# One attention and int8 feed-forward layer on 8 cores: normalising block kg+1 ahead of the key/value work of block kg, or right before its own

## The reference, cut to what matters

```python
x = L0_attn_x                                  # (4, 4096, 2048) f32
x = x + layernorm(attn(layernorm(x)))
x = x + layernorm(ffn(layernorm(x)))

def attn(x, Wq, bq, Wdown, Wk_up, Wv_up, Wo, bo):   # 16 heads of 128
    q = x @ Wq + bq
    kv_latent = x @ Wdown                      # 2048 -> 512
    k = kv_latent @ Wk_up                      # 512 -> 2048
    v = kv_latent @ Wv_up
    ...                                        # rotary embedding on q and k
    scores = q k^T / sqrt(128), causal mask, softmax, times v
    return ctx @ Wo + bo

def ffn(x):                                    # int8 weights, 2048 -> 8192 -> 2048
    return qmatmul(silu(qmatmul(x, w_gate, s_gate)) * qmatmul(x, w_up, s_up),
                   w_down, s_down)
```

## Time and profile before

| what | us |
|---|---|
| runs shown: lowest, median, highest of 3 | 6573.32, 7085.65, 7111.39 |
| profiled execution, its time | 6567.78 |
| its span on the slowest core (core 3) | 6566.2 |
| its spans on all cores | 6519.4 to 6566.2 |

### The profile page before, as it was taken

One profiled execution on the slowest core, in us unless ns is written; L12 is line 12 of the kernel. 1 busy time (PEld: TensorE's weight loads), 2 busy tenths in 40 slices (PEclk: granted clock), 3 DMA queues, 4 the chain that ended last, 5 costly groups with the idle time before them and its releaser, 6 DMA issues.

```text
span 6566.2 us, 67793 instructions; the slowest of 8 cores (6519.4 to 6566.2 us)
## 1 busy us (share of the span) xinstructions
PE 4422.5 (67%) x21376; PEld 2017.3 (31%) x21376; DVE 1584.4 (24%) x2965; ACT 1349.6 (21%) x3067; POOL 818.8 (12%) x924
## 2 busy tenths in 40 slices
PE   0144334486666666663334999789986999879986
PEld 0011111132333334331111443334432444334432
DVE  0142334244333333323332110121102111021101
ACT  0212221111666666521111110010000110011100
POOL 0021112243000000000000111111111111111111
PEclk9867667798767776676666999989998999989998
DMA  9423333532777777764437996499946997489944
GB/s 180 114 77 109 90 95 90 126 79 78 153 147 150 147 148 147 149 151 128 140 119 144 154 154 136 120 177 151 154 129 153 151 151 137 128 161 151 160 119 131
DMA packets 1566328, 883.21 MB, mean 135 GB/s; under 512 B 777122, under 2 KB 1541026, under 8 KB 1550242
## 3 DMA queue, kind: packets, MB, share of 16 engines
q0 software_dynamic: 679296, 434.14, 39.1%
q1 hardware_dynamic: 839842, 327.28, 22.6%
q10 hardware_dynamic: 46848, 117.45, 5.3%
HBM read 398.53 MB, written 109.05 MB: 77 GB/s over the span
## 4 chain that ended last, share of the span: by engine, by line
PE 45%; DMA 19%; DVE 11%; ACT 10%; issue 8%; POOL 3%; SPq 2%; another core or an unknown queue 1%; ACTq 1%; DVEq 0%; POOLq 0%
PE ps L1031 14%; PE ps L1045 13%; PE ps L1098 7%; DMA arena<-wd 7%; ACT arena L766 7%; DMA ctxr<-xin 4%; PE ps L864 3%; PE ps L442 2%; PE ps L738 2%; DMA arena<-arena 2%; DVE smalls L760 2%; POOL arena L621 2%; PE ps L699 2%; DMA arena<-wo 1%; DVE arena L477 1%
## 5 line engine op out<-in xcount | busy, mean ns | idle before, releaser
L1031 PE MATMUL ps<-arena 128*128 128x512 bf16 x4096 | 936.2, 382 | 259.9 <-DMA arena<-wg 137.9
L1098 PE MATMUL ps<-arena 128*128 128x512 bf16 x4096 | 920.3, 380 | 140.1 <-DMA arena<-wd 138.7
L1045 PE MATMUL ps<-arena 128*128 128x512 bf16 x4096 | 925.8, 379 | 0.0
L766 ACT ACTIVATE arena<-ps,smalls 128x512 bf16<-128x512 f32 (+1 forms) x1152 | 748.9, 669 | 469.7 <-DVE smalls L760 322.8
L738 PE MATMUL ps<-arena 128*128 128x512 bf16 (+1 forms) x1152 | 488.3, 486 | 415.1 <-ACT arena L766 336.9
L1031 PEld LDWEIGHTS ps<-arena 128*128 128x128 bf16 x4096 | 403.0, 98 | 752.0 <-issue 275.6
L411 PE MATMUL ps<-arena 128*128 128x512 bf16 x512 | 130.4, 420 | 693.6 <-ACT arena L420 452.6
L1098 PEld LDWEIGHTS ps<-arena 128*128 128x128 bf16 x4096 | 385.7, 98 | 674.0 <-issue 246.5
L1061 DVE TENSOR_SCALAR ctxr<-ps,smalls 128x512 bf16<-128x512 f32 x256 | 192.1, 751 | 1498.7 <-PE ps L1045 1498.7
L1045 PEld LDWEIGHTS ps<-arena 128*128 128x128 bf16 x4096 | 400.8, 98 | 483.3
L1056 ACT ACTIVATE ctxr<-ps,smalls 128x512 bf16<-128x512 f32 x256 | 176.1, 688 | 1562.4 <-PE ps L1031 1562.3
(11 more groups left out here) (74 smaller groups left out, 2785.6 us busy)
## 6 DMA issues: line engine op xcount, KB each, us to landing
arena<-wg POOLq DMA_DIRECT2D x128, 1024.0 KB, 7.3
arena<-wu POOLq DMA_DIRECT2D x128, 1024.0 KB, 7.3
arena<-wd POOLq DMA_DIRECT2D x256, 512.0 KB, 3.8
ctxr<-xin SPq DMA_DIRECT2D x32, 1024.0 KB, 6.0
arena<-wo_scr ACTq DMA_DIRECT2D x16, 2048.0 KB, 9.4
xnf_scr<-arena SPq DMA_DIRECT2D x16, 1024.0 KB, 7.1
k_scr<-ctxr SPq DMA_DIRECT2D x16, 1024.0 KB, 7.1
v_scr<-ctxr SPq DMA_DIRECT2D x16, 1024.0 KB, 7.4
```

What stands on the lines that cost most here:

```text
L766: s.activation(P_b[par][:, n0:n0 + N], psa[:, 0:N], ACT.Exp, bias=negc[:, par:par + 1], scale=1.0, accum_out=lacc[:, par * 8 + ci: par * 8 ...
L1031: rr = t.matmul(ga, wg_s[slp][:, fc, icw * 128:(icw + 1) * 128], x1nfm[:, fc, :], start=(fc == 0), stop=(fc == NH - 1))
L1045: rr = t.matmul(ua, wu_s[slp][:, fc, icw * 128:(icw + 1) * 128], x1nfm[:, fc, :], start=(fc == 0), stop=(fc == NH - 1))
L1098: rr = t.matmul(psa, f_b[:, quar * 4 + ic, j * 128:(j + 1) * 128], wd_s[qp][:, ic, :], start=(quar == 0 and ic == 0), stop=(quar == 15 and ...
```

## The change

The call of `front(0)` ahead of the loop is gone, and the loop calls `front(kg)` and `back(kg)` of one and the same block. The functions themselves are untouched; the number of instructions on each engine stays the same.

```diff
-        front(0)
         for kg in range(NKG):
-            if kg + 1 < NKG:
-                front(kg + 1)
+            front(kg)
             back(kg)
```

## The result

Against the kernel before, the changed kernel's time has the ratio 1.013 (95% interval 1.011 to 1.015). The profiled execution took 6646.3 us; before it was 6567.78 us. The median of ten runs is 7111.67 us beside 6684.71 us, and this pair can't be read as the change: in more than half of the executions of either kernel (15 of 28 before, 10 of 16 changed, over all comparisons here) the cores of one die or of both show a lower granted clock and the time is some per cent longer, so a median of ten falls on one side or the other by chance.

What follows compares the result with a forecast made beforehand. Phase A was taken as bound by front and back running one after the other, 130.6 us a block. Seven backs +77.7, last block +8.0, front(1) −4.4: +81 us on 6567.8, 6649 us; range 6600 to 6710 us.

Steps and rivals of the forecast that it cites:

- (1): Phase A, start of a block's latent matmuls: the first waits for the fourth transpose to land, 4.7 us; +4.1 us a block.
- (2): Phase A, latent matmuls: all 64, not 32, lie on the path behind the wait, 16.35 us; +7.0 us a block.
- (3): Phase A, K, V and the stores: same instructions with the same neighbours, cost 0; 52.2 us in the last block.
- (4): Phase A, last block: front(7) now comes right before back(7), which takes 74.05 us, before 66.1; +8.0 us.
- (5): Phase A, front(1): it now follows V stores like the six others, 70.4 us, before 74.8; −4.4 us.
- Rival 3: Phase E: its waits for `wg` and `wd` shrink and take the delay back, 6568 us or less; chance 5%.
- Rival 4: Phase A: every front takes 74.8 us in place of 70.4, 35 us more, 6684 us; chance 5%.
- Rival 1: Phase A: fronts really ran beside backs, so calling them late costs 430 us, about 7000 us; chance 2%.
- rival 2: Phase A: bursts of 64 latent matmuls stay at the slow clock, 27.5 us, 89 us more, 6738 us; chance 6%.

## Why the prediction was right, and where it was off

**Forecast.** The prediction said 6649 us on the base of the profiled execution, +1.2%; the changed kernel's profiled execution took 6646.3 us, and the ratio is 1.013. The mechanism is the one that was described. That the whole agrees within 3 us is partly luck: phase A grew by 75.8 us and not 81, and the rest of the program, unchanged, took 10.7 us more in this execution. Step by step, by the mean of the cores:

- Steps (1) and (2), landing and two more latent chunks: forecast +11.1 us a block. Measured +10.6 from V stores to V stores in the changed kernel (132.1 to 142.7). Each part alone: +6.5 for the chunks with the earlier release, expected +6.3; the landing 4.6 us more (138.6 to 143.3), expected 4.8. The landing was 4.5 us in the rows above (375.34 to 379.85), the lower bound, not 4.7; the burst 16.0 us in the mean of the eight (15.33 to 16.70), not 16.35.
- Step (3), K and V at no cost: holds. In the last block before, 52.2 us lay between the first K matmul and the V stores; in block 1 of the changed kernel it is 51.8, from the end of the burst and 0.8 us of cast (396.0) to the stores at 447.80.
- Steps (4) and (5), from the fourth transpose's issue to the V stores and from the V stores to the fourth transpose, in the same means. Back(7) went from 66.2 to 73.7 us, +7.5 (forecast +8.0), and front(1) from 74.1 to 69.4, −4.6 (forecast −4.4). Backs 0 to 6 went from 62.8 to 73.6, +10.8 each. The rest is in the other seven fronts, which were forecast at no change and are 2.6 us shorter in all. The sum of phase A thus was 81 in the forecast and 75.8 in the traces. The forecast was worked out on core 3, whose phase A before was 11.5 us longer than the mean (1078.8 to 1067.3); so its last V stores "to about 1323" came at 1303.5 in the rows above.
- The barrier passes it all on: the wait before phase B is 86.0 us, before 84.5 by the window and 85.3 by the wait.
- Rival 3: the waits for `wg` and `wd` went from 277 to 282 us. Nothing was taken back. Rival 4: fronts of 69.9 us in the rows above and 69.0 in the mean of all cores and of fronts 1 to 7, not 74.8. Rival 1: V stores stand 142 us apart, not 190.

**Where it was wrong.** Two steps of the last part failed, and neither is about the mechanism. The first is the base: "I forecast on the base of the profile, as my terms do", with a range of 6600 to 6710 us. Two of the three times shown, 7085.65 and 7111.39, already lay over 500 us above that base; the +81 us held (75.8 in phase A, 78.5 in the profiled execution), but the 6567.8 us that it was added to lay below all three times shown. The measured median, 7111.67, lies 402 us above the top of my range. The figure of 7167 us which I worked out from the median of three and laid aside was nearer, but by chance too: over ten runs the median before was 6684.71. The second is "A measurement of this kernel can tell about 2%": the comparisons tell 0.2 to 0.3% (the half widths of the two intervals), and twice the same size came out, 1.013 and 1.0127, with intervals that leave out 1. A loss of 1.3% is therefore seen as a loss; the 88% for "within 2%" came true, but says nothing of it.

**Also read wrongly:** rival 2 got 6% against rows that excluded it already; the seven bursts of 32 had all finished in 8.4 to 10.0 us.

## What to carry to other kernels

Calling a stage one step ahead and giving it double buffers is no overlap where each engine works through its list in order: look at the period. If it is the sum of the two stages, as here (69 + 61.5 us in 130.6), moving the whole call changes only what slips through at the seam, 11 us a block; overlap has to be written into the lists, piece by piece, and here that was worth 5.8%, with the loads two tiles ahead, while the leading call was worth 1.3%. First look at what each load stands behind on its queue: in the changed order, the few lines that put two loads ahead of the V stores gave 22 us a block.

## What the runs showed that I had not expected

- The leading call of the kernel before is worth its 11 us a block though nearly all of it is serial, and one added wait gives it up whole.
- The latent burst with no idle time before it, or up to 2.2 us of it, and at a granted clock of 1.00, is 13.97 to 13.98 us in five different kernels (the last block of three, the interleaved one and the one with the extra matmuls); behind 52 us of idle time or more it is 15.3 to 16.9. Eighty unread matmuls remove that on six cores, two others lose by them in three blocks, and the whole time doesn't show the gain.
- The 5.3 ms behind phase A vary by up to 21 us in the mean of the cores between executions of one and the same code. A difference of 30 us is read more safely from the phase in which it arises than from two whole times.
